# The first edge list sorted in two halves, the in-direction in two passes, and GpSimd's indirect DMAs held to two in flight

## The chip, the cores and the metric

The kernel runs on 1 core of one Trainium2 chip. The metric is the device time of one execution in microseconds, as the median of several runs.

## The reference, cut to what matters

A layer over a graph of 6250 nodes and 100000 edges, then a mixture of six experts. `hidden` is the layer-normalised x:

```python
def _srgnn_conv(x, W, b, src, dst, num_nodes):
    xl = x @ W.T + b
    msgs = xl[src]
    agg = jax.ops.segment_sum(msgs, dst, num_segments=num_nodes)
    cnt = jax.ops.segment_sum(jnp.ones((src.shape[0],), x.dtype), dst, num_segments=num_nodes)
    return agg / jnp.maximum(cnt, 1.0)[:, None]
input_in = _srgnn_conv(hidden, W_in, b_in, src, dst, n)
input_out = _srgnn_conv(hidden, W_out, b_out, dst, src, n)
gi = jnp.concatenate([input_in, input_out], axis=-1) @ W_ih.T + b_ih
gh = hidden @ W_hh.T + b_hh
# three gates from gi and gh (sigmoid, sigmoid, tanh) give the new rows
x = x + gru(gi, gh, hidden)
x = x + experts(_layernorm(x))   # 6 experts, the best 2 of each token
```

## The kernel before, in words

Everything is written out for the engines by hand, with semaphores; each engine runs its own list of instructions in order.

Nodes are padded to 6400 = 50 buckets (`NB`) of 128. Edges are 782 tiles (`TILES`) of 128, in room for 784 slots (`NS`); `HS` = 392 is half of that. For each direction the kernel needs the edges in the order of the receiving node. `positions(d)` (VectorE L900 and L942, TensorE L1553 and L1580) works out the place of each edge. A place is a slot (a tile) and a row in it. Then the list is written into order in one of two ways:

- A **sort tile**: VectorE builds a one-hot of the rows times the payload (L974, two of 128x128) and, VectorE (L978) or ScalarE (L614), a step over the slots (128x788). TensorE adds rows x steps into PSUM, 4 matmuls of 393 columns a tile (L1600). `decode` takes differences of neighbouring columns and gets the entries back.
- A **scatter**: GpSimd writes 128 entries into a list in DRAM by an indirect DMA (L392).

The list of direction 0 (the in-direction) takes 448 tiles (`SORTED_TILES`) by a loop of sort tiles, 112 groups of 4, and 336 by scatters, beside positions(1); SP reads the scattered list back and `decode(0)` adds both. The list of direction 1 is sorted inside the in-direction, three sort tiles a visit.

Then each direction gathers and sums. GpSimd gathers the 128 sender rows of a tile by an indirect DMA into a ring (L431, 782 a direction). Four tiles are a batch. A bucket may begin in the middle of a batch, so TensorE makes 245 **visits** (batch, bucket) a direction. In a visit VectorE builds the one-hot of the four tiles (L1070), and TensorE multiplies it with each tile's rows (L1674, 512 columns, the high and the low halves of the values) and with ones for the count (L1675). `bucket_mean` ends a bucket: ScalarE scales the high half (L606 `hi_mean`), VectorE adds the low half (L1100, L1171).

In the out-direction each bucket is followed by the products of the gates and the routing for that tile, and the experts come last, with 108 gathers (L448) and 108 adding scatters (L459) of GpSimd.

TensorE's sequencer runs register instructions (addresses that depend on loop counters) and waits between the matmuls. GpSimd's gathers wait for `slot_done`, which a visit's last matmul signals.

Of the kernel before, what the change touches and what calls it, by code (L numbers as in the profile page):

```python
# [13 lines left out]
F32 = mybir.dt.float32  # L14
# [26 lines left out]
VISITS = BATCHES - 1 + NB  # L41
KEY = 256
SORTED_TILES = 448
TILES = -(-EDGES // P)
VISIT_TILES = 3
GROUP = 4
# [5 lines left out]
SORT_GROUPS = SORTED_TILES // GROUP  # L52
# [3 lines left out]
ACT_TILES = (1, 3)  # L56
LIST = 2 * NS * P
# [14 lines left out]
MORE = TILES - VISITS * VISIT_TILES  # L72
# [13 lines left out]
assert MORE == NB - 3 and SORT_GROUPS % SETS == 0 and NB % 4 == 2  # L86


def gnn_moe_program(nc, x, edges, w, out, table, lists, means, routed):
    ctx = ExitStack()  # L90
    with ctx:
# [41 lines left out]
        def twin_sb(name, shape):  # L133
# [18 lines left out]
        bucket_base = sb("bucket_base", [P, 1], F32)  # L152
        base_digit = sb("base_digit", [P, 2], F32)
        base_row = carve("sort", [2 * HALF])
        count_digits = sb("count_digits", [P, 2], F16)
        bucket_i = sb("bucket_i", [P, 4], I32)
# [7 lines left out]
        slot_of, row_of, pay_hi, pay_lo = [[carve(user, [NS]) for user in ("sort", "live")] for _ in range(4)]  # L164
        list_at = carve("sort", [NS], I32)
        payload = carve("sort", [2, NS], I32)
        raw_list = list_at
        late = at["live"]
        step_gap = carve("live", [NS])
        first_slot = sb("first_slot", [P, 2], F32)  # L170
        first_place = sb("first_place", [P, 2], F32)
        first_batch = sb("first_batch", [1, 2, 64], I32)
        first_row = carve("sort", [64], I32)
# [7 lines left out]
        assert 4 * (at["live"] - LIVE) - 2 * 4 * NS >= WIDE_RING * 4 * D  # L181
# [22 lines left out]
        ring = sb("ring", [P, RING, 2 * D], F16)  # L204
        rings = (ring[:], over(region_at + 4 * LIVE, [WIDE_RING, 2 * D], F16))
# [93 lines left out]
        names = ("consts const_step spread_ready edges_in ln_mean ln_stats rows_scaled h_ready hi_ready split_ready table_stored "  # L299
                 "dve_step onehot_ready onehot_used slots16_ready slot_prefix_ready base_ready "  # L300
                 "list_at_ready list_zeroed list_in  merged sort_ready sort_used sort_summed column_ready half_ready receivers_ready "
                 "decoded  turn owners_marked owners_summed rows_landed slot_done "
                 "node_onehot_used key_ready node_onehot_ready bucket_done inv_ready hi_mean_ready "
# [8 lines left out]
        ln_in = [sem(f"ln_in{i}") for i in range(2)]  # L312
        spill_landed = [sem(f"spill_landed{i}") for i in range(2)]
        x_landed = [sem(f"x_landed{i}") for i in range(2)]
        S = {n: sem(n) for n in names}
        scatter_landed = sem("scatter_landed")
# [3 lines left out]
        N_CONSTS = 21  # L320
        sums, counts = (banks[4], banks[6]), (banks[5], banks[7])
        sort_hi, sort_lo = banks[0:2], banks[2:4]
        owners = banks[4:6]
# [12 lines left out]

        block = ctx.enter_context(nc.Block())

        @block.gpsimd
        def _(pool):  # L340
            g = nc.gpsimd
            c = S["consts"]
# [12 lines left out]
            g.memset(first_batch[:], BATCHES - 1).then_inc(c, 1)  # L355
# [32 lines left out]
            pool.wait_ge(S["list_zeroed"], 12 * 16)  # L388
            pool.wait_ge(S["list_at_ready"], 1)

            for t_ in range(SORTED_TILES, NS):
                g.indirect_dma_start(  # L392
                    out=lists[0][:], out_offset=bass.IndirectOffsetOnAxis(ap=list_at[:, t_:t_ + 1], axis=0),
                    in_=payload[:, 0, t_:t_ + 1], in_offset=None,
                ).then_inc(scatter_landed, 16)

# [25 lines left out]
            for d in range(2):  # L422
                pool.wait_ge(S["decoded"], 2 * d + 1)
                for i in range(TILES):
                    if i == LEAD:
                        pool.wait_ge(S["decoded"], 2 * d + 2)
# [13 lines left out]
            pool.wait_ge(S["iters_ready"], 1)  # L440
            pool.wait_ge(S["xn_landed"], (NB // 2 + 1) * 16)
# [3 lines left out]
            def gather_tokens(i):  # L445
                par, k = i // STREAMS % 2, i % STREAMS
                for h in range(2):
                    g.indirect_dma_start(  # L448
                        out=rows[:, par, k, h, :], out_offset=None, in_=routed[:],
                        in_offset=bass.IndirectOffsetOnAxis(ap=token[:, 2 * i + h:2 * i + h + 1], axis=0),  # L450
                    ).then_inc(rows_in[par][k], 16)

            def add_results(i):
# [4 lines left out]
                for h in range(2):  # L458
                    g.indirect_dma_start(  # L459
                        out=out[:], out_offset=bass.IndirectOffsetOnAxis(ap=token[:, 2 * i + h:2 * i + h + 1], axis=0),  # L460
                        in_=result[:, i % STREAMS, h, :], in_offset=None, compute_op=ALU.add,
                    ).then_inc(S["added"], 16)
# [10 lines left out]
        def _(sp):  # L473
# [6 lines left out]
            entries = lists[0].rearrange("(p n) o -> p (n o)", p=P)[:, 0:NS]  # L480
            for q in range(4):
                sp.dma_start(entries[:, q * (NS // 4):(q + 1) * (NS // 4)],
                             zeros16[:, 0:NS // 2].bitcast(I32)).then_inc(S["list_zeroed"], 16)

            for q in range(2):
                sp.dma_start(means[NP + q * P:NP + q * P + P, :], zeros16[:].bitcast(F32)
                             ).then_inc(S["list_zeroed"], 16)
                sp.dma_start(out[NP + q * P:NP + q * P + P, :], zeros16[:].bitcast(F32)
                             ).then_inc(S["list_zeroed"], 16)
                sp.dma_start(routed[NP + q * P:NP + q * P + P, 0:D], zeros16[:].bitcast(F32)  # L490
                             ).then_inc(S["list_zeroed"], 16)
                sp.dma_start(routed[NP + q * P:NP + q * P + P, D:ROW], zeros16[:, 0:2 * (ROW - D)].bitcast(F32)
                             ).then_inc(S["list_zeroed"], 16)
# [14 lines left out]

            sp.wait_ge(scatter_landed, (NS - SORTED_TILES) * 16)
            sp.dma_start(raw_list, entries).then_inc(S["list_in"], 16)  # L510
            sp.wait_ge(S["list_in"], 16)

            sp.wait_ge(S["decoded"], 2)
            sp.dma_start(r_w1, w["r_w1"].rearrange("(c p) n -> p c n", p=P)).then_inc(S["experts_in"], 16)
            sp.dma_start(e_b3.rearrange("p e d -> p (e d)"), w["e_b3"].to_broadcast([P, NE * D])).then_inc(S["experts_in"], 16)
            for n, name in enumerate(("e_w1", "e_w2", "e_w3")):
                sp.dma_start(e_w[n].rearrange("p e c m -> p (e c) m"), w[name].rearrange("e (c p) n -> p (e c) n", p=P)
                             ).then_inc(S["experts_in"], 16)
            for d in range(2):
# [7 lines left out]
                with sp.Fori(0, whole) as r:  # L527
                    for k in range(parts):
                        landed(r, k)
# [5 lines left out]
        def _(act):  # L535
# [68 lines left out]
            def hi_mean_step(q, k):  # L604
                act.wait_ge(S["inv_ready"], q)
                a.activation(hi_mean[:], sums[k][:, 0:D], ACT.Copy, scale=inv_count[:, 1:2]  # L606
                             ).then_inc(S["hi_mean_ready"], 1)

# [4 lines left out]
            def slot_steps(d, t, out_):  # L613
                a.activation(out_, iota_half, ACT.Sign, scale=-1.0, bias=slot_of[d][:, bass.ds(t, 1)]  # L614
                             ).then_inc(S["column_ready"], 1)

            act.wait_ge(S["half_ready"], 1)
            act.wait_ge(S["merged"], 2 * NB + 4)
            with act.Fori(0, SORT_GROUPS // SETS) as r:
                for g_ in range(SETS):  # L620
                    act.wait_ge(S["sort_used"], r * SETS + (g_ + 1))
                    act.sem_inc(S["turn"], 1)
                    for k in ACT_TILES:
                        slot_steps(0, r * SORT_BUFS + (g_ * GROUP + k), slot_step[:, g_ * GROUP + k, :])
            act.wait_ge(S["decoded"], 2)

            def spill_mean(j, k):
                hi_mean_step(j + 1, k)
# [4 lines left out]
            def visit_step(j, b, past):  # L633
                at_ = b + j
                act.wait_ge(S["node_onehot_used"], at_ + (OH + 1 - SETS))
                act.sem_inc(S["turn"], 1)
                slot_steps(1, at_ * VISIT_TILES + (past + 1),
                           slot_step[:, bass.ds(at_ * GROUP % SORT_BUFS + 1, 1), :].rearrange("p a m -> p (a m)"))

            def bucket_steps(j, k, more, later=True):  # L640
                act.sem_inc(S["turn"], 1)
                lo = act.value_load(first_batch[0:1, 0, bass.ds(j, 1)], min_val=0, max_val=BATCHES - 1)
                hi = act.value_load(first_batch[0:1, 0, bass.ds(j + 1, 1)], min_val=0, max_val=BATCHES - 1)
                past = j + 1 if more else MORE
                visit_step(j, lo, past)
                if later:
                    spill_mean(j - 1, 1 - k)
                act.sem_inc(S["turn"], 1)
                with act.If(hi > lo):
                    with act.Fori(lo + 1, hi + 1) as b:  # L650
                        visit_step(j, b, past)
# [1315 lines left out]
```

## Time and profile before

| what | value |
|---|---|
| median of 3 runs | 3091.45 us (3090.6 to 3100.2) |
| span of the profiled execution | 4434.5 us |
| mean granted clock of TensorE in it | 0.808 |

The profiled execution is known by its span alone, which is 1343 us over the median of the runs. Parts of it: the front with positions and scatters up to about 560 us, the sort loop up to about 880, the in-direction up to about 2300, the out-direction up to about 3950, the experts to the end.

### The profile page before, as it was taken

To read this page: it belongs to the slowest core of one execution; us is meant where nothing else is said; L and a number is where in the kernel's file an instruction comes from. 1 tells how busy PE (TensorE), PEld (TensorE's weight loads), DVE (VectorE), ACT (ScalarE), POOL (GpSimd) and SP (SyncE) were. 2 spreads that over 40 slices of the span, in tenths; PEclk is the share of its full clock that TensorE was granted. 3 is DMA by queue.
4 is the path that set the end of the run, shared out by engine and by line. 5 is a ranking of instruction groups with operands and counts; after the bars stand their busy time and mean duration, and the time that the engine had idled before them with its cause. 6 is when DMAs were issued, how large, how long until landed. Compare 5 with 4: busy or idle time off the path is not lost. (4 is left out here: it accounts for less than half of the span.)

```text
span 4434.5 us, 68226 instructions
## 1 busy us (share of the span) xinstructions
PE 2745.1 (62%) x14312; PEld 1616.8 (36%) x14313; DVE 2093.1 (47%) x6910; ACT 908.1 (20%) x1572; POOL 2164.5 (49%) x2165
## 2 busy tenths in 40 slices
PE   5211159977777777777764555555555555566896
PEld 2100025533333333333322333333333333345775
DVE  8201179975565556655552333443333433354221
ACT  4100026631112111111110010110111101112443
POOL 0777700035665555655645444444444444433786
PEclk9655589988888888888877777777777777787998
DMA  3100000022222222222222222222222222212444
GB/s 116 30 24 24 18 16 0 0 95 80 86 81 82 78 79 81 79 83 81 84 72 83 77 82 72 74 79 74 83 72 76 75 75 82 71 60 45 80 80 61
DMA packets 178175, 298.24 MB, mean 67 GB/s; under 512 B 51779, under 2 KB 123460, under 8 KB 178118
## 3 DMA queue, kind: packets, MB, share of 16 engines
q0 software_dynamic: 106560, 234.06, 19.8%
q10 hardware_dynamic: 44790, 35.90, 2.6%
q1 hardware_dynamic: 26768, 27.70, 2.0%
q14 instruction: 43, 0.35, 0.0%
q8 instruction: 14, 0.23, 0.0%
HBM read 255.56 MB, written 41.94 MB: 67 GB/s over the span
## 5 line engine op out<-in xcount | busy, mean ns | idle before, releaser
L431 POOL DMA_INDIRECT ring<-split_rows,live x782 | 791.5, 1012 | 923.4 <-DVE live L1035 381.8
L431 POOL DMA_INDIRECT over<-split_rows,gather_row x782 | 747.5, 956 | 933.0 <-PE bank L1674 681.5
L1600 PE MATMUL bank<-over,over 128*128 (+1 forms) x4920 | 1008.9, 354 | 143.1 <-issue 123.6
L1600 PEld LDWEIGHTS bank<-over,over 128*128 (+1 forms) x4920 | 485.9, 102 | 597.7 <-issue 351.9
L974 DVE TENSOR_SCALAR over<-iota_cols,live,live 128x128 f16 x1564 | 411.4, 319 | 119.9 <-issue 113.1
L392 POOL DMA_INDIRECT list<-sort,sort x336 | 332.7, 990 | 218.3 <-issue 111.0
L1674 PE MATMUL bank<-ring,dense 128*128 x980 | 329.5, 430 | 126.7 <-issue 100.1
L1714 PE MATMUL bank<-dense,dense 128*128 128x512 f32 (+1 forms) x600 | 262.0, 437 | 184.5 <-DVE dense L1183 174.1
L1675 PE MATMUL bank<-ones_col,dense 128*128 128x1 f16 x1960 | 334.9, 171 | 2.7 <-issue 2.5
L1674 PE MATMUL bank<-over,dense 128*128 x980 | 277.7, 386 | 94.5 <-issue 77.8
L614 ACT ACTIVATE over<-live,live 128x788 f16 x245 | 221.6, 945 | 492.2 <-remote 271.7
L606 ACT ACTIVATE hi_mean<-bank,inv_count 128x256 f32<-128x256 f32 x100 | 47.4, 474 | 1331.4 <-DVE inv_count L1097 586.9
L1733 PE MATMUL bank<-ident,mean_b 128*128 128x128 f32 x100 | 30.4, 400 | 432.5 <-DVE mean_b L1171 345.3
L1161 DVE TENSOR_SCALAR inv_count<-bank 128x1 f32<-128x1 f32 x50 | 7.9, 158 | 586.9 <-remote 536.7
L614 ACT ACTIVATE over<-live,sort 128x788 f16<-128x788 f16 x224 | 200.6, 944 | 200.7 <-DVE sort L942 102.9
L1715 PE MATMUL bank<-w_gate_low,dense 128*128 128x512 f32 (+1 forms) x600 | 239.7, 400 | 0.0
L978 DVE TENSOR_SCALAR over<-iota_cols,live 128x788 f16 x537 | 230.1, 428 | 19.3 <-issue 18.6
L1716 PE MATMUL bank<-dense,dense 128*128 128x512 f32 (+1 forms) x600 | 238.0, 397 | 0.0
L1070 DVE TENSOR_TENSOR dense<-live,node_key 128x512 f32 x245 | 168.9, 689 | 138.6 <-issue 51.1
L974 DVE TENSOR_SCALAR over<-iota_cols,sort,sort 128x128 f16<-128x128 f16 x896 | 227.1, 308 | 13.9 <-DVE live L965 0.5
L1714 PEld LDWEIGHTS bank<-dense,dense 128*128 128x128 f32 x600 | 146.2, 244 | 217.7 <-DVE dense L1183 180.0
L1889 PE MATMUL bank<-over,over 128*128 128x256 f32 x864 | 204.8, 401 | 29.7 <-issue 27.3
(304 smaller groups left out, 3927.7 us busy)
## 6 DMA issues: line engine op xcount, KB each, us to landing
norm<-in_x SPq DMA_DIRECT2D x20, 640.0 KB
ring<-split_rows,live POOLq DMA_INDIRECT x782
over<-split_rows,gather_row POOLq DMA_INDIRECT x782
split_rows<-over SPq DMA_DIRECT2D x10, 640.0 KB
in_edge_means<-dense ACTq DMA_DIRECT2D x50, 128.0 KB
dense<-in_x ACTq DMA_DIRECT2D x50, 128.0 KB
dense<-in_edge_means ACTq DMA_DIRECT2D x50, 128.0 KB
out<-dense ACTq DMA_DIRECT2D x25, 256.0 KB
```

What stands on the lines that cost most here:

```text
L392: g.indirect_dma_start(out=lists[0][:], out_offset=bass.IndirectOffsetOnAxis(ap=list_at[:, t_:t_ + 1], axis=0), in_=payload[:, 0, t_:t_ + ...
L431: g.indirect_dma_start(out=rings[d][:, i % ring_slots[d], :], out_offset=None, in_=table[:], in_offset=bass.IndirectOffsetOnAxis(ap=gather ...
L614: a.activation(out_, iota_half, ACT.Sign, scale=-1.0, bias=slot_of[d][:, bass.ds(t, 1)]).then_inc(S["column_ready"], 1)
L974: ins = e.tensor_scalar(rows_(half), iota_cols[:, 0:P], row_of[d][:, bass.ds(t, 1)], pay[:, bass.ds(t, 1)], ALU.is_equal, ALU.mult)
L978: ins = e.tensor_scalar(slots, iota_cols[:], slot_of[d][:, bass.ds(t, 1)], 2.0, ALU.is_le, ALU.mult)
L1600: ins = t.matmul(bank[h][:, 0:HS + 1], rows_(half), slots(h), start=False, stop=False, skip_group_check=True)
L1674: summed = t.matmul(sums[k][:, :], oh, rows, start=False, stop=False, skip_group_check=True)
L1675: ins = t.matmul(counts[k][:, 0:1], oh, ones_col[:], start=False, stop=False, skip_group_check=True)
L1714: t.matmul(o, a_hi, b_hi, start=first, stop=False, skip_group_check=True)
L1715: t.matmul(o, a_hi, b_lo, start=False, stop=False, skip_group_check=True)
L1716: return t.matmul(o, a_lo, b_hi, start=False, stop=last, skip_group_check=True)
L1889: ins = t.matmul(stream_bank[k][:, m * 2 * P:(m + 1) * 2 * P], w_stage[:, k, n_, c, m * P:m * P + P], right[:, k, c, :], start=(c == 0), s ...
```

## The change

- No scatters. The list of direction 0 is sorted in two halves of 392 slots each. A sort tile of it takes two matmuls of 393 columns. The first 392 tiles are sorted in a loop (`half_group`, 98 groups of 4) ahead of the in-direction.
- The in-direction is made in two passes of 147 visits each, 294 in all. Pass 0 works on the first half of the list, and meanwhile the other 390 tiles (`late_groups`, `late_tiles`, `late_steps`: 10 for each of the first 39 buckets) are sorted; decode(1) and receivers(1) follow in pass 0. Pass 0 writes a bucket's sums to DRAM (`bucket_part`, `spill_part`), pass 1 loads and completes them (`load_part`, `bucket_mean`).
- Pass 0 sorts two tiles of direction 1 a visit, pass 1 three.
- A sort tile's payload rows are built by one instruction of 128x256. In the half loop three of four slot steps are ScalarE's.
- A visit's two halves of the values are added in PSUM: per tile a matmul of 256 columns and one of 257, where the last column is a one that stands in the ring; no L1675, and no `hi_mean` in the out-direction.
- `few_queued`: each indirect DMA of GpSimd waits until the last but one has left its engine.

The core of the diff:

```diff
-SORTED_TILES = 448
+HALF_TILES = TILES - HS
 VISIT_TILES = 3
+EARLY_TILES = 2
+BUCKET_TILES = 10
-ACT_TILES = (1, 3)
+ACT_TILES = (1, 2, 3)
+SLOT = 2 * D + 8
+SENT_AHEAD = 2
...
+            def few_queued():
+                issued[0] += 1
+                if issued[0] > SENT_AHEAD:
+                    pool.wait_ge(S["sent"], issued[0] - SENT_AHEAD)
...
+                    if d == 0 and i == HS:
+                        pool.wait_ge(S["decoded"], 3)
                     if i % BATCH == 0 and i >= ring_slots[d]:
                         pool.wait_ge(S["slot_done"], d * NS + i + BATCH - ring_slots[d])
+                    few_queued()
                     g.indirect_dma_start(
-                        out=rings[d][:, i % ring_slots[d], :], out_offset=None, in_=table[:],
+                        out=rings[d][:, i % ring_slots[d], 0:2 * D], out_offset=None, in_=table[:],
                         in_offset=bass.IndirectOffsetOnAxis(ap=gather_row[d][:, i:i + 1], axis=0),
+                        engine_sem=S["sent"],
                     ).then_inc(ring_landed[d][i // BATCH % (ring_slots[d] // BATCH)], 16)
...
+            def sort_rows(d, t, rows_):
+
+                return e.scalar_tensor_tensor(
+                    out=two(rows_), in0=iota_cols[:, 0:P].rearrange("p (o m) -> p o m", o=1).to_broadcast([P, 2, P]),
+                    scalar=row_of[d][:, bass.ds(t, 1)],
+                    in1=pay[d][:, bass.ds(t, 1), :].rearrange("p t (a o) -> p (t a) o", o=1).to_broadcast([P, 2, P]),
+                    op0=ALU.is_equal, op1=ALU.mult)
...
+            def half_products(rows_, slots):
+                for bank, half in ((half_hi, 0), (half_lo, 1)):
+                    ins = t.matmul(bank[:, 0:HS + 1], rows_(half), slots, start=False, stop=False,
+                                   skip_group_check=True)
+                return ins
...
+            def late_groups(j):
+                for q in range(BUCKET_GROUPS):
+                    for i in range(2):
+                        pe.wait_ge(S["half_ready"], j * BUCKET_TILES + (HS + 2 * q + i + 1))
+                        pe.wait_ge(S["half_column"], j * BUCKET_TILES + (HALF_GROUPS * len(ACT_TILES) + 2 * q + i + 1))
+                        pe.sem_inc(S["turn"], 1)
+                        buf = late_buffer(j * BUCKET_GROUPS + q, i)
+                        ins = half_products(lambda half: row_payload[:, buf, half * P:half * P + P
...
                     for q in range(BATCH):
...
+                        for lo_, hi_ in ((0, D), (D, 2 * D + 1)):
...
                     if d == 0:
-                        for i in range(VISIT_TILES):
-                            ins = sort_tile(at_ * VISIT_TILES + (past + i), i, at_)
+                        for i in range((EARLY_TILES, VISIT_TILES)[p]):
+                            ins = sort_tile(visit_tile(p, at_, past) + i, i, at_)
```

GpSimd's instructions ahead of and at the start of the gathers, before the change (`list` is the list in DRAM, `split_rows` the table of rows, `sort_79` and `live_82` the buffers with the places):

```order
L385 AFFINE_SELECT spread_base<-spread_base 128x50 [waits spread_ready]
L392 DMA list<-sort_79,sort_78 200704x1 [waits list_at_ready,list_zeroed]
L392 DMA list<-sort_79,sort_78 200704x1 x335
L431 DMA ring<-split_rows,live_82 128x512 [waits decoded,fold_done,table_stored]
L431 DMA ring<-split_rows,live_82 128x512 x15
L431 DMA ring<-split_rows,live_82 128x512 [waits slot_done]
```

and the same place after it (`sent` is the new semaphore, `slot_done` frees the ring):

```order
L409 AFFINE_SELECT spread_base<-spread_base 128x50 [waits spread_ready]
L439 MEMSET ring 128x16 [waits decoded,fold_done,table_stored]
L450 DMA ring<-split_rows,live_79 128x512 x2
L450 DMA ring<-split_rows,live_79 128x512 [waits sent] x14
L450 DMA ring<-split_rows,live_79 128x512 [waits sent,slot_done]
L450 DMA ring<-split_rows,live_79 128x512 [waits sent] x3
```

The 336 scatters are gone, and each gather has a wait for `sent` of its own beside the wait for the ring at every fourth.

The first two of the four edge tiles in TensorE's visit, in the in-direction, before (`ring` is the gathered rows, `dense_104` the one-hots; ISA is a register instruction):

```order
L1688 ISA
L1674 ISA [waits node_onehot_ready,rows_landed]
L1674 ISA
L1674 MATMUL bank<-ring,dense_104 128x512
L1675 MATMUL bank<-ones_col,dense_104 128x1
L1674 ISA
L1674 MATMUL bank<-ring,dense_104 128x512
L1675 MATMUL bank<-ones_col,dense_104 128x1
```

and after:

```order
L1841 ISA
L1825 ISA [waits node_onehot_ready,rows_landed]
L1825 ISA
L1825 MATMUL bank<-ring,dense_101 128x256
L1825 ISA
L1825 MATMUL bank<-ring,dense_101 128x257
L1825 ISA
L1825 MATMUL bank<-ring,dense_101 128x256
L1825 ISA
L1825 MATMUL bank<-ring,dense_101 128x257
```

Five register instructions stood at the products of a visit, and nine stand there now, one ahead of each matmul; the two matmuls of a tile have 256 and 257 columns for 512 and 1.

## Rows read from the trace of the kernel before

**Rows 1.** Head of the page: span; engine, busy us (share), instructions.

```profile
span 4434.5 us, 68226 instructions
...
PE 2745.1 (62%) x14312; PEld 1616.8 (36%) x14313; DVE 2093.1 (47%) x6910; ACT 908.1 (20%) x1572; POOL 2164.5 (49%) x2165
```

**Rows 2.** Table by stretches: busy us of each engine, granted clock, DMA share, GB/s.

```profile
core 0: us, PE busy (x) PEld busy (x) DVE busy (x) ACT busy (x) POOL busy (x), PEclk, DMA share, GB/s
...
114.00:340.00 226.00, 42.78 (x140) 18.06 (x138) 34.57 (x82) 26.70 (x46) 170.21 (x173) 0.57 0.10 27
340.00:560.00 220.00, 26.50 (x79) 10.67 (x79) 35.22 (x61) 15.28 (x24) 162.51 (x164) 0.52 0.08 21
...
660.00:880.00 220.00, 220.00 (x1312) 127.04 (x1310) 209.23 (x827) 147.03 (x164) 0.00 (x0) 1.00 0.00 0
...
1000.00:2200.00 1200.00, 900.73 (x4678) 411.83 (x4675) 700.46 (x2310) 223.94 (x265) 710.70 (x701) 0.86 0.28 81
...
2400.00:3900.00 1500.00, 821.80 (x4458) 549.58 (x4458) 592.73 (x2187) 167.39 (x348) 667.49 (x700) 0.78 0.25 77
```

**Rows 3.** Waits from 114 to 560 us: line <- releaser, us in total, times, longest.

```profile
DVE over L900 <- remote: 168.5, 9, 21.0
...
DVE sort L942 <- remote: 127.6, 7, 19.5
```

**Rows 4.** Waits from 2400 to 3900 us, the same columns.

```profile
POOL over L431 <- PE bank L1674: 640.8, 47, 16.3
DVE inv_count L1161 <- remote: 522.1, 41, 18.6
```

**Rows 5.** Order of time, 2996 to 3012 us: start, duration, instruction, idle before, releaser.

```profile
2997.97 0.27 PE L1735 MATMUL bank<-ident,flags 128*128 128x128 f32 x1
...
3006.70 0.95 POOL L431 DMA_INDIRECT over<-split_rows,gather_row  x1 [0.30 <-issue]
3010.27 0.42 DVE L1180 CAST dense<-bank 128x256 fp32r<-128x256 f32 x1 [9.81 <-remote]
```

**Rows 6.** Line L392: count, shortest/median/longest ns, first and last start.

```profile
L392 POOL DMA_INDIRECT list<-sort,sort x336: 954/962/2474, 114.7 to 557.4; - x168
```

**Rows 7.** GpSimd in order of time, two neighbours: start, duration.

```profile
300.29 0.95 POOL L392 DMA_INDIRECT list<-sort,sort  x1 [0.30 <-issue]
301.55 0.96 POOL L392 DMA_INDIRECT list<-sort,sort  x1 [0.30 <-issue]
```

**Rows 8.** The page's groups for two sort steps: count | busy us, mean ns | idle.

```profile
L614 ACT ACTIVATE over<-live,sort 128x788 f16<-128x788 f16 x224 | 200.6, 944 | 200.7 <-DVE sort L942 102.9
...
L974 DVE TENSOR_SCALAR over<-iota_cols,sort,sort 128x128 f16<-128x128 f16 x896 | 227.1, 308 | 13.9 <-DVE live L965 0.5
```

**Rows 9.** Line L1100: count, shortest/median/longest ns.

```profile
L1100 DVE SCALAR_TENSOR_TENSOR dense<-bank,inv_count,hi_mean x50: 482/483/485, 984.0 to 2298.5; 128x256 f32<-128x256 f32 x50
```

**Rows 10.** TensorE in order of time, one visit of the in-direction.

```profile
1283.01 0.39 PE L1674 MATMUL bank<-ring,dense 128*128 x1 [0.48 <-issue]
...
1283.99 2.17 PE L1600 MATMUL bank<-over,over 128*128 x12
1286.59 0.39 PE L1674 MATMUL bank<-ring,dense 128*128 x1 [0.42 <-issue]
```

**Rows 11.** TensorE in order of time, one visit of the out-direction.

```profile
2712.84 0.39 PE L1674 MATMUL bank<-over,dense 128*128 x1 [0.44 <-issue]
...
2714.39 0.39 PE L1674 MATMUL bank<-over,dense 128*128 x1 [0.44 <-issue]
```

**Rows 12.** Line L1674: shortest/median/longest ns, first and last start.

```profile
L1674 PEldq FUSED_REGOPS  x2450: 3/74/1374, 957.8 to 3987.5; - x189
...
L1674 PE MATMUL bank<-ring,dense x980: 376/377/634, 958.1 to 2294.9; 128*128 x196
...
L1674 PE MATMUL bank<-over,dense x980: 376/376/607, 2314.4 to 3988.1; 128*128 x196
```

**Rows 13.** TensorE's groups, 1000 to 2200 us: busy us, mean ns | idle before.

```profile
L1600 PE MATMUL bank<-over,over 128*128 x2802 | 632.1, 367 | 126.0 <-issue 112.8 <-DVE over L978 7.2 <-DVE over L974 2.3
...
L1657 PE MATMUL bank<-zeros 128*128 128x512 f16 x44 | 21.9, 499 | 65.6 <-issue 65.6
```

**Rows 14.** The page's groups for the gathers and for hi_mean.

```profile
L431 POOL DMA_INDIRECT ring<-split_rows,live x782 | 791.5, 1012 | 923.4 <-DVE live L1035 381.8
...
L606 ACT ACTIVATE hi_mean<-bank,inv_count 128x256 f32<-128x256 f32 x100 | 47.4, 474 | 1331.4 <-DVE inv_count L1097 586.9
```

More of the change, by code:

```diff
@@ L526, in _ @@
                 whole = (BATCHES - 1) // parts
-                with sp.Fori(0, whole) as r:
+                begun = 0
+                if d == 0:
+                    begun = -(-HALF_BATCHES // parts)
+                    with sp.Fori(0, begun) as r:
+                        for k in range(parts):
+                            landed(r, k)
+                    load_experts()
+                with sp.Fori(begun, whole) as r:
                     for k in range(parts):
@@ L641, in bucket_steps @@
+            def bucket_steps(p, j, k, pair=0, more=False, half=False, later=True):
                 act.sem_inc(S["turn"], 1)
[L642 to L643 removed]
+                lo = act.value_load(first_batch[0:1, p, bass.ds(j, 1)], min_val=0, max_val=BATCHES - 1)
+                hi = act.value_load(first_batch[0:1, p, bass.ds(j + 1, 1)], min_val=0, max_val=BATCHES - 1)
@@ L650, in bucket_steps @@
                     with act.Fori(lo + 1, hi + 1) as b:
-                        visit_step(j, b, past)
-            bucket_steps(0, 0, True, False)
+                        visit_step(p, j, b, past)
+            bucket_steps(0, 0, 0, half=True, later=False)
+            for first, last, half in ((0, HALF_BUCKETS // 2, True), (HALF_BUCKETS // 2, NB // 2 - 1, False)):
+                with act.Fori(first, last) as r:
+                    for k in (1, 0):
+                        bucket_steps(0, r * 2 + (2 - k), k, r, half=half)
+            bucket_steps(0, NB - 1, 1, NB // 2 - 1)
+            spill_part(NB - 1, 1, NB // 2 - 1)
+            for k in range(2):
+                act.wait_ge(spill_landed[k], NB // 2 * 16 + 16)
+            bucket_steps(1, 0, 0, more=True, later=False)
             for n_ in range(4):
@@ L931, in positions @@
-                e.tensor_copy(first_slot[:, d:d + 1], bucket_i[:, 1:2])
-                e.tensor_copy(first_place[:, d:d + 1], bucket_i[:, 2:3])
+                                              prefix[:, HS - 1:HS] if h and d else 0.0, ALU.mult, ALU.add))
+                for n_ in range(parts):
+                    end = NS - 1 if n_ == parts - 1 else HS - 1
+                    ins = e.tensor_copy(bucket_i[:, n_:n_ + 1], prefix[:, end:end + 1])
+                step(ins)
+                e.tensor_single_scalar(bucket_i[:, 2:2 + parts], bucket_i[:, 0:parts], 7, ALU.arith_shift_right)
@@ new lines, in positions @@
+                for n_ in range(parts):
+                    hi_at, lo_at = n_ * HALF, (parts + n_) * HALF
+                    ins = e.scalar_tensor_tensor(out=first_row[0:1, n_, 0:NB], in0=base_row[0:1, hi_at:hi_at + NB],
+                                                 scalar=float(P), in1=base_row[0:1, lo_at:lo_at + NB],
+                                                 op0=ALU.mult, op1=ALU.add)
+                step(ins)
+                if d == 0:
+                    step(e.tensor_single_scalar(first_row[0:1, 0, 0:NB], first_row[0:1, 0, 0:NB],
+                                                float(HS * P - 1), ALU.min))
@@ new lines, in decode, with receivers @@
+                v.wait_ge(S["decoded"], (2, 3, 5)[p])
+            def receivers(p):
+                d = p // 2
+                s2 = decode_rooms[d][2]
+                v.wait_ge(S["owners_summed"], p + 1)
+                for h, bank in enumerate(owners[p]):
+                    at_ = HS if p == 1 else h * HS
+                    step(e.scalar_tensor_tensor(out=receiver[d][:, at_:at_ + HS], in0=bank[:, 0:HS],
+                                                scalar=float(KEY), in1=s2[:, at_:at_ + HS], op0=ALU.mult, op1=ALU.add))
@@ L1130, in _ @@
             e.memset(bias_pack.bitcast(F32), 0.0).then_inc(S["bias_clear"], 1)
-            bucket_a(0, True)
+            bucket_a(0, False)
+            for n_ in range(4):
+                with v.Fori(EARLY_PAIRS[n_], EARLY_PAIRS[n_ + 1]) as r:
+                    for k in (1, 0):
+                        next_bucket(0, r * 2 + (2 - k), k, r, half=n_ == 0)
+                if n_ == 1:
+                    decode(1)
+                if n_ == 2:
+                    receivers(1)
+            next_bucket(0, NB - 1, 1, NB // 2 - 1)
+            bucket_part(NB - 1, 1, NB // 2 - 1)
+            bucket_a(1, True)
             for n_ in range(4):
```

613 lines of the change are left out of this document (344 added, 269 removed).

## Prediction

> **What bounds the kernel now.** I read the head of the page first: the profiled execution took 4434.5 us, TensorE was busy for 62% of it and GpSimd for 49% [rows 1]. The median of the runs shown is 3091.45 us, 1343 us less. No engine fills the span, so I went to the table by stretches [rows 2]. The reader is to see two kinds of stretch there. From 660 to 880 us TensorE is busy for all of its 220 us at a granted clock of 1.00: the sort loop. From 114 to 560 us, where GpSimd issues the scatters, TensorE, VectorE and ScalarE together are busy for 42.8 + 34.6 + 26.7 + 26.5 + 35.2 + 15.3 = 181 us of 446. So for at least 265 us none of the three works. In the out-direction, 2400 to 3900 us, TensorE has 822 us of 1500.
>
> The waits say what stands there. In the scatter stretch VectorE's L900 and L942 wait 168.5 and 127.6 us for a releaser on another engine that the trace does not place, up to 21.0 us at a time [rows 3]. In the out-direction VectorE's L1161 waits 522.1 us in the same way, and GpSimd's gathers 640.8 us for the matmuls that free the ring [rows 4]. One place shows the pattern: TensorE's L1735 starts at 2997.97 and lasts 0.27 us; VectorE's L1180, which needs only that product, starts at 3010.27 after 9.81 us of idling, and in between GpSimd goes through one gather after another until its last at 3006.70 [rows 5]. TensorE's signal comes through late while GpSimd has indirect DMAs queued. That is what holding the DMAs back would act on.
>
> **How the profiled time stands to the timed one.** Take out the 265 us and the 522 us, and add that without the first the sort loop would run beside the scatters and not after them (another 300 us). Those three are 1087 of the 1343 us by which the profiled execution is longer, and the in-direction's own stretch (from 958.1 to 2294.9 [rows 12], 1337 us, against about 1000 us by the price of its parts, below) covers the rest. So the timed runs cannot hold much of these late signals: what is left without them is about the median. I therefore make the sum for the timed runs from the durations of undisturbed stretches, start at 3091, and treat late signals in the timed runs as a rival.
>
> **Front: scatters out, half a list in.** The scatters run from 114.7 us, 336 of them [rows 6], one each 1.26 us by two neighbours [rows 7], so 425 us: they end at 540 (in the trace, with some longer ones, the last starts at 557.4). Beside them positions(1) should take about as long as positions(0), which was done with the load and the layer norm by 114.7: 125 us, to 240. The sort loop issues 1312 matmuls in the full 220 us, 16 a group, so 2.68 us a group [rows 2]; 112 groups are 300 us, to 540. Both paths end together there. After the change the scatters, their landing and the read-back are gone, and the loop has 98 groups. The new row builder is one scalar_tensor_tensor of 128x256. Nothing in the trace is the same operation; the nearest are L1100, 128x256 from PSUM at 0.483 us, and the pair of tensor_scalars that it replaces at 227.1/896 = 0.253 us each, 0.51 us a pair [rows 8, 9]. A group costs VectorE 4 x 0.40 to 0.48 plus one step of half the width, about 0.2 us: 1.8 to 2.1 us. ScalarE's three half-width steps are 3 x 0.944/2 = 1.42 us, TensorE's eight matmuls 1.34. So 98 x 1.85 = 181 us, to about 420: **-120 us** (-95 to -130). The first decode handles half the columns: **-10**.
>
> **In-direction: 294 visits for 245, and 390 late tiles.** At full clock a visit starts at 1283.01, its four edge tiles end at 1283.99, the twelve sort matmuls take 2.17 us, and after 0.42 us of idle "issue" the next starts at 1286.59: 3.58 us [rows 10]. In the out-direction, with no sort tiles, visits stand 1.55 us apart with 0.44 us of "issue" [rows 11]. So each visit has about 0.43 us in which the array waits for its sequencer. At L1674 the trace has 2450 register instructions for 490 visits, five a visit, with a median of 74 ns [rows 12]; after the change the code has nine. Four more at 0.074 us are 0.30 us; in proportion to the gap they are 4 x 0.43/5 = 0.34, which I take (an estimate; nothing if matmuls cover them).
>
> Before: 245 x 3.58 = 877, 50 bucket turns of 1.5 us (65.6 us of idle in 44 at L1657 [rows 13]) 75, 49 extra sort tiles 33: 985 us. GpSimd's 782 gathers at 1.012 us plus 0.30 of issue make 1026 at most, or 990 at the usual 0.96 [rows 7, 14]. The two are even; I take 1000.
>
> After, pass 0: a visit has two sort tiles, 3.58 - 0.68 + 0.34 = 3.24 us, 147 of them 476. A late tile has two matmuls of 393 columns, 0.34 us at the rate of the sort tiles, and its own waits and register work, between nothing and 0.45 us; half of that gives 0.57, 390 of them 222. Turns 75. Sum 773. Pass 1: 147 x 3.92 = 576, 47 extra tiles 32, turns 75: 683. Together 1456, **+456**. With no register time added, 147 x 2.90 + 133 + 75 and 147 x 3.58 + 32 + 75: 634 + 633 = 1267, +267. If no idle "issue" shows at all, visits of 3.15 and two fewer for a sort tile: about 1140, +140. A longer bucket turn points up: at its end a sort matmul waits 126.0 us in all [rows 13], 2.9 us a bucket; if that is of the turn, 50 more turns add 143. VectorE, busy for 700.5 of 1200 us with three sort tiles a visit [rows 2], gets two in pass 0 and 390 x 0.48 = 187 us of late rows; GpSimd needs 391 x 1.26 = 493 us a pass. Neither becomes the bound. I take **+370**, between the two values that keep the gap seen in rows 10.
>
> [...] The trace shows 1.5 us of a turn without work for the array at L1657 [rows 13]; it doesn't show what the sequencer does in it. [...]
>
> **Out-direction and experts.** hi_mean's ACT step (0.474 us, 50 of its 100 [rows 14]) leaves the chain: -24. The visits get the same four register instructions: 245 x 0.34 = +83 if TensorE is the limit there; it is busy for 822 of 1500 us, and the chain through VectorE and ScalarE decides part of it. I take **+20** (-24 to +60). The hold on GpSimd costs nothing as long as two DMAs in flight keep it busy: 1.26 us apart, with 0.30 of it issue.
>
> Sum: 3091 - 120 - 10 + 370 + 20 = 3351, **3350 us**. In a profile the late signals should go: the front ends near 440 us where it ended at 880, the in-direction is 1456 - 1337 = 120 us longer, and the out-direction about 500 shorter. Its span should fall to 4434 - 440 + 120 - 500, about 3610 us, although the timed runs get longer.
>
> **Rivals.**
> 1. Faster: late signals are in the timed runs too. 787 us of them are in the trace (265 and 522). The change loses 260 by my sum, so the balance turns where a third of the 787 is in the timed runs; with half, 3350 - 394 = 2956 us. For it: the hold acts on just that pattern, and the scatters that caused the first part are gone. Against it: the accounting above leaves little room for them in 3091 us. Chance 0.22.
> 2. Faster or no change: TensorE's register work is hidden. Then the in-direction costs +140, the out-direction -24: 3091 - 130 + 140 - 24 = 3077; with gathers that the profile slows, even less. For it: TensorE's share of the in-direction is 75% by the table (900.7 of 1200 us). Against: the gap stands in each full-clock visit. Chance 0.16, 0.09 of it faster.
> 3. Slower still: the hold makes GpSimd wait for a late signal of its own. If each indirect DMA starts 0.30 us later, a pass of 391 is 610 us, still under TensorE's; in the out-direction 782 x 0.30 = +235 at most: 3585. Against: a limit of two leaves the next one queued. Chance 0.05.
> 4. My forecast, chance 0.57.
>
> **How the numbers follow.** About 0.3% (9 us) is what a measurement of this kernel can tell from no change. Slower: 0.57 + 0.05 = 0.62. Faster: 0.22 + 0.09 = 0.31. Same: the other 0.07 of rival 2. The forecast's own range is 3190 (in-direction +210) to 3500 (+500 with longer turns). The whole range goes down to 2930, where rival 1 has half of the late signals, and up to 3500.
>
> **What would show it.** In the profile after: no long VectorE waits without a placed releaser in the front; the half sort loop at about 1.85 us a group and done some 120 us sooner after positions(1); full-clock visits at about 3.2 and 3.9 us with 0.7 to 0.8 us of "issue"; late tiles at 0.57 us; the two passes together over 1300 us; gathers still 1.26 us apart. The forecast is wrong if visits without sort work keep 1.55 us, if both passes together are near 1050 us, or if the timed median falls although the passes are long: then the late signals were in the timed runs.

## The result, and the profile after

The changed kernel takes 3616.3 us (median of 4 runs, 3609.5 to 3621.3) where the kernel before takes 3091.0 us: a ratio of 1.169, with an interval of 1.1665 to 1.1712. It is 525 us slower. The direction was forecast and the size was not: 260 us were forecast, and the time lies outside the range.

The head of the page of the changed kernel, and its two groups of gathers:

```profile
span 3619.3 us, 77644 instructions
...
PE 2775.0 (77%) x14673; PEld 1664.5 (46%) x14674; DVE 2141.5 (59%) x6095; ACT 1100.0 (30%) x2031; POOL 1921.9 (53%) x1832
...
L450 POOL DMA_INDIRECT ring<-split_rows,live x782 | 857.2, 1096 | 815.1 <-PE bank L1825 333.6
L450 POOL DMA_INDIRECT over<-split_rows,gather_row x782 | 772.5, 988 | 241.8 <-DMA over<-split_rows,gather_row 184.2
```

The span is 3619 us, and this time it is the time of the runs too. The span before was 4434 us against runs of 3091 [rows 1]. So the two pages can't be subtracted: they would show a kernel that became 815 us faster. What the profile of before was is the first thing to find out (e0, e1 below). In the first group the gathers of the in-direction stand idle for 815 us, in the second one for 242.

The changed kernel by stretches. They are cut at the zeroing products of TensorE that open a bucket, so that they are the front, pass 0 (25 buckets with gathers, then 13 with late tiles alone, then the last 12), pass 1 (24 buckets without gathers, then 26 with), and the out-direction; the experts follow to the end:

```profile
core 0: us, PE busy (x) PEld busy (x) DVE busy (x) ACT busy (x) POOL busy (x), PEclk, DMA share, GB/s
0.00:444.00 444.00, 324.82 (x1476) 118.86 (x1478) 414.16 (x935) 263.93 (x581) 18.29 (x45) 0.93 0.18 57
444.00:1093.00 649.00, 495.72 (x2504) 238.26 (x2501) 340.75 (x813) 240.85 (x372) 382.39 (x384) 0.95 0.29 83
1093.00:1258.00 165.00, 110.69 (x492) 46.64 (x492) 85.70 (x219) 79.62 (x142) 0.00 (x0) 0.93 0.03 10
1258.00:1329.00 71.00, 46.16 (x221) 23.95 (x221) 33.16 (x89) 9.81 (x11) 12.93 (x14) 0.83 0.39 125
1329.00:1526.00 197.00, 128.65 (x622) 68.41 (x623) 109.43 (x332) 38.45 (x48) 2.47 (x3) 0.85 0.11 34
1526.00:2134.00 608.00, 475.05 (x2615) 258.63 (x2613) 377.33 (x968) 128.40 (x156) 455.63 (x383) 0.94 0.33 94
2134.00:3190.00 1056.00, 854.34 (x5179) 621.36 (x5179) 674.83 (x2469) 167.36 (x343) 767.53 (x790) 0.94 0.41 121
```

The in-direction runs from 444 to 2134 us, 1690 us. From 1093 to 1526 us GpSimd has 17 instructions, 14 of them ahead of pass 1: the edges come sorted by receiver, so the first half of the list has the edges of the first 24 buckets and part of the 25th alone. Pass 0 finds no gathers for the last 25, and pass 1 none for the first 24; each of them still gets a visit.

### The profile page after: what moved, and what is told of

It is laid out like the page before. It is cut to its first block and busy times, and to the rows that moved or that the text cites. A ratio compares the mean times of both kernels' runs of the same rounds, so it can differ in the third digit from the quotient of the medians.

```text
span 3619.3 us, 77644 instructions
## 1 busy us (share of the span) xinstructions
PE 2775.0 (77%) x14673; PEld 1664.5 (46%) x14674; DVE 2141.5 (59%) x6095; ACT 1100.0 (30%) x2031; POOL 1921.9 (53%) x1832
## 5 line engine op out<-in xcount | busy, mean ns | idle before, releaser
L1716 PE MATMUL bank<-over,over 128*128 x3128 | 633.4, 346 | 84.1 <-DVE over L1049 44.9
L1730 PE MATMUL bank<-over,over 128*128 128x393 f16 (+1 forms) x1564 | 396.3, 362 | 143.0 <-issue 118.7
L1042 DVE SCALAR_TENSOR_TENSOR over<-iota_cols,sort,sort 128x256 f16<-128x256 f16 (+1 forms) x782 | 333.3, 497 | 250.7 <-PE bank L1730 250.0
L634 ACT ACTIVATE over<-live,sort 128x393 f16 (+1 forms) x684 | 368.9, 613 | 320.3 <-PE bank L1730 270.6
L1716 PEld LDWEIGHTS bank<-over,over 128*128 x3128 | 310.2, 100 | 336.0 <-issue 246.4
L1825 PEld LDWEIGHTS bank<-ring,dense 128*128 x2352 | 232.4, 99 | 353.3 <-issue 256.0
L1042 DVE SCALAR_TENSOR_TENSOR over<-iota_cols,live,live 128x256 f16 x782 | 362.1, 478 | 31.0 <-PE bank L1716 29.4
L1825 PEld LDWEIGHTS bank<-over,dense 128*128 x1960 | 199.7, 102 | 290.8 <-issue 205.9
L1730 PEld LDWEIGHTS bank<-over,over 128*128 128x128 f16 (+1 forms) x1564 | 124.2, 98 | 414.1 <-issue 310.5
L483 POOL DMA_INDIRECT out<-over,dense x108 | 173.4, 1606 | 79.7 <-ACT over L869 22.8
```

The source lines that it names most:

```text
L634: a.activation(out_, iota_half[:, 0:number], ACT.Sign, scale=-1.0, bias=slot_of[d][:, bass.ds(t, 1)]).then_inc(ready, 1)
L1042: return e.scalar_tensor_tensor(out=two(rows_), in0=iota_cols[:, 0:P].rearrange("p (o m) -> p o m", o=1).to_broadcast([P, 2, P]), scalar=r ...
L1716: ins = t.matmul(bank[h][:, 0:HS + 1], rows_(half), slots(h), start=False, stop=False, skip_group_check=True)
L1730: ins = t.matmul(bank[:, 0:HS + 1], rows_(half), slots, start=False, stop=False, skip_group_check=True)
L1825: ins = t.matmul(bank[:, 0:hi_ - lo_], oh, rows, start=False, stop=False, skip_group_check=True)
```

## The experiments

The kernel before was timed again beside each group of runs, with medians from 3091 to 3104 us. So a difference in us between two kernels of different groups is good to about 12 us; the ratios are each to the kernel before of the same group.

**e0: the kernel before, profiled once more.**

> The kernel before once more, for its profile. If queued indirect DMAs of GpSimd always delay TensorE's signals in a profiled execution, the span is again near 4430 us with VectorE's long unplaced waits. If that was a matter of the one execution shown, the span is near 3100, and the hold had nothing to take away.

Its span is 3093.3 us. Head of its cores, then its stretches, cut as above: in-direction from 582 to 1626, where the first bucket of the out-direction is opened, out-direction to 2664, experts:

```profile
core 0: 3093.3 us, clock 0.941
```

```profile
582.00:1626.00 1044.00, 848.17 (x5247) 428.89 (x5248) 763.82 (x2621) 251.89 (x301) 787.20 (x784) 0.98 0.38 110
1626.00:2664.00 1038.00, 844.68 (x5030) 562.27 (x5028) 675.64 (x2454) 190.52 (x389) 768.65 (x790) 0.93 0.41 123
2664.00:3093.00 429.00, 338.55 (x1574) 287.64 (x1574) 109.12 (x288) 172.62 (x384) 283.79 (x216) 0.88 0.42 68
```

No wait in it is put down to a releaser that the trace does not place. VectorE's longest in the out-direction (1700 to 2600 us) is now short, and for TensorE:

```profile
DVE inv_count L1161 <- PE bank L1691: 106.2, 43, 6.4
```

The late signals of [rows 3 to 5] belonged to the one profiled execution shown. A second profiled execution of the same kernel, at 3093.3 us, has none. All comparisons from here are with this trace. In it the gathers of both directions run back to back (the page's groups):

```profile
L431 POOL DMA_INDIRECT ring<-split_rows,live x782 | 786.2, 1005 | 245.1 <-issue 234.1
L431 POOL DMA_INDIRECT over<-split_rows,gather_row x782 | 774.3, 990 | 256.3 <-issue 232.7
```

That is 786 + 245 = 1031 us for each direction, nearly all of it without a wait for another engine. So the gathers set the pace of both directions. In the in-direction TensorE is close behind: it waits 39.8 us for gathered rows (the releaser is SP, which passes their landing on), and GpSimd 4.0 us for it:

```profile
PE bank L1674 <- SPq L524: 39.8, 44, 4.6
POOL ring L431 <- PE bank L1674: 4.0, 13, 0.3
```

**e1 and e2: the hold alone, and the change without it.** Each has the hold's two lines put in or taken out at each indirect DMA; e1:

```diff
+                    few_queued()
                     g.indirect_dma_start(
...
+                        engine_sem=S["sent"],
```

> The kernel before with the hold of the change alone, on its scatters, gathers and the experts' DMAs. If the added 525 us are the two passes' own work and the late signals belong to the profiled execution alone, the timed median stays within 1% of 3091 us, and the profiled span comes down to about it, with the in-direction at about 1000 us and the scatters ending near 540. If the hold is what costs, the timed median goes up by 150 to 300 us. If late signals are in the timed runs as well, it falls below 3000.

> The changed kernel without the hold. If the passes cost and the hold is free, the timed median stays within 1% of 3616 us while the profiled span goes back up, to over 4000. If the hold costs, the timed median falls to about 3350, my forecast. If late signals matter in timed runs, it rises.

e1: 3103.6 us, a ratio of 1.0032 (1.0014 to 1.005). e2: 3612.0 us, 1.1661 (1.1627 to 1.1694), which overlaps that of the change. Its profiled span is 3610 us, not over 4000 as I expected: without the hold there are no late signals either. So the hold costs 4 to 15 us of the kernel before and gives nothing back; all but that of the 525 us is the rest of the change. The rival that the hold costs is out.

**e4: four more register instructions a visit, in the kernel before.**

```diff
-                        rows = batches[:, bass.ds(part, 1), q * 2 * D:(q + 1) * 2 * D].rearrange("p a m -> p (a m)")
-                        summed = t.matmul(sums[k][:, :], oh, rows, start=False, stop=False, skip_group_check=True)
+                        for lo_, hi_ in ((0, D), (D, 2 * D)):
+                            part_rows = batches[:, bass.ds(part, 1), q * 2 * D + lo_:q * 2 * D + hi_].rearrange("p a m -> p (a m)")
+                            summed = t.matmul(sums[k][:, lo_:hi_], oh, part_rows, start=False, stop=False,
+                                              skip_group_check=True)
```

> The kernel before with the hold, and each 512-column product of a visit made as two of 256 columns, each with its own register instruction: four more register instructions and four more matmuls a visit in both directions, 490 visits. If register instructions cost what I took (0.34 us a visit), the in-direction gets 83 us longer and the out-direction up to 83: 90 to 170 us over the kernel with the hold alone. If they are hidden, within 30 us of it.

3220.0 us, 116 over e1. The zeroing products of two neighbouring buckets, in e0 and in e4 (last two times: first and last start):

```profile
L1657 PE MATMUL bank<-zeros x2: 387/388/388, 707.7 to 728.3; 128*128 128x512 f16 x2
```

```profile
L1672 PE MATMUL bank<-zeros x2: 387/388/388, 817.0 to 840.1; 128*128 128x512 f16 x2
```

A bucket of the in-direction goes from 20.6 to 23.1 us, 0.5 us for each of its 4.9 visits. The array has the same columns to take in, so this is the price of four matmuls and their register instructions in TensorE's own row; no run parts the two. It is not hidden there, and it is more than the 0.34 us of the forecast. From the first zeroing product to the first of the out-direction e1 takes 1043 us and e4 1149:

```profile
L1672 PE MATMUL bank<-zeros x51: 377/387/607, 583.1 to 1626.4; 128*128 128x512 f16 x51
```

```profile
L1672 PE MATMUL bank<-zeros x51: 383/388/608, 584.6 to 1733.8; 128*128 128x512 f16 x51
```

That is 106 us of the 116 (less than 245 x 0.5, since e1's TensorE has waits for gathered rows to give away: 33.9 us in e1, 4.8 in e4). What follows, with the same four more a visit in the out-direction, gets about 6 us longer (3215.3 - 1733.8 for 3102.1 - 1626.4). From the first gather of the out-direction to the last it is 1014 us in e4 and 1017 in e1: behind the gathers the four more are hidden.

**e3 and e8: without the late tiles,** in the changed kernel and in the spread one:

```diff
             def late_groups(j):
+                return
...
-                    pe.wait_ge(S["half_used"], HALF_GROUPS + SETS + HALF_BUCKETS * BUCKET_GROUPS)
+                    pe.wait_ge(S["half_used"], HALF_GROUPS + SETS)
```

and the same `return` in `late_tiles` and `late_steps`.

> The changed kernel without the 390 late tiles: the second half of the list is left out, so pass 1 sums wrong rows. The trace of the changed kernel has a late tile each 0.76 us where it stands alone. If TensorE's row of late tiles is the bound, 390 x 0.76 = 296 us go: about 3320. By my forecast's price of 0.57 it would be 222 us. If they lay beside other work, under 100 us go.

> The spread kernel without its 390 late tiles: the second half of the list is left out, so pass 1 sums wrong rows. If late tiles are fully on the path when the work is spread, 296 us under the spread kernel. If they fall behind the gathers (391 x 1.32 = 516 us a pass), under 200.

e3: 3458.0 us, 158 less; neither number that I gave. In its trace the first 25 buckets fall from 26.3 to 21.5 us only, since there the gathers are next in line (15.6 a bucket, some 20.6 us by the 1031 us for 782), and the later buckets of pass 1, whose gathers all read one row here, take 27.4 us for 23.5, for a reason that is not settled. e8, where no bucket has more gathers than TensorE's work covers, is cleaner: 3251.1 us, 286 under e5. A late tile costs 286/390 = 0.73 us, near the 0.76 of the trace and not the 0.57 of the forecast.

**e5: the tiles dealt out to the halves.**

```diff
-    edges = _np.ascontiguousarray(edges.reshape(2, NS, P).transpose(2, 0, 1))
+    order = [*range(0, TILES - 1, 2), TILES - 1, *range(1, TILES - 1, 2), TILES, TILES + 1]
+    edges = _np.ascontiguousarray(edges.reshape(2, NS, P)[:, order].transpose(2, 0, 1))
```

> The changed kernel with the tiles of the input list dealt out alternately to the two halves (an order of the array on the host), so that each pass has gathers for all 50 buckets; before it the first 25 buckets had all of pass 0's gathers, since the list comes sorted by receiver. Visits and sort tiles stay in number. If GpSimd's standing idle through the single-visit buckets is the loss (25 x 5.3 + 25 x 8.3 = 340 us), the time falls by 200 us or more. If TensorE's count of visits, late tiles and turns is the bound in every bucket, passes of 147 x 3.39 + 390 x 0.76 + 50 x 2 = 894 and 147 x 3.92 + 32 + 50 x 2.5 = 733 follow: about 60 us less, 3550.

3537.3 us, ratio 1.1387 (1.1364 to 1.1411): 79 less, near the 3550 of the theory that TensorE's count of things is the bound, and far from the 200 or more of the other. Bucket openings in pass 0 of the changed kernel (with gathers and late tiles; late tiles alone; neither), in pass 1 (without gathers; with), then of the spread kernel in pass 0 and 1, and of e8 in pass 0:

```profile
L1805 PE MATMUL bank<-zeros x3: 272/272/272, 889.4 to 942.0; 128*128 128x257 f16 x3
L1805 PE MATMUL bank<-zeros x4: 272/272/272, 1092.8 to 1130.8; 128*128 128x257 f16 x4
L1805 PE MATMUL bank<-zeros x4: 273/282/376, 1258.4 to 1274.2; 128*128 128x257 f16 x4
L1805 PE MATMUL bank<-zeros x4: 282/282/283, 1402.2 to 1427.0; 128*128 128x257 f16 x4
L1805 PE MATMUL bank<-zeros x2: 281/282/282, 1631.7 to 1655.2; 128*128 128x257 f16 x2
```

```profile
L1805 PE MATMUL bank<-zeros x3: 272/272/272, 615.0 to 653.8; 128*128 128x257 f16 x3
L1805 PE MATMUL bank<-zeros x3: 281/282/283, 1389.0 to 1418.5; 128*128 128x257 f16 x3
```

```profile
L1808 PE MATMUL bank<-zeros x3: 281/281/282, 604.3 to 628.0; 128*128 128x257 f16 x3
```

The buckets of the changed kernel take 26.3, 12.7, 5.3, 8.3 and 23.5 us; in the spread one 19.4 and 14.8, and 11.9 without late tiles. In a spread pass GpSimd has about 8 gathers a bucket, some 10 us at 1031/782 us each, so it sets no bucket's time. GpSimd's pause in the changed kernel is mostly a consequence: what TensorE does in it would have to be done at another time anyway.

**e7 and e9: late tiles' waits once a pair,** in the changed kernel and in the spread one.

```diff
-                    for i in range(2):
-                        pe.wait_ge(S["half_ready"], j * BUCKET_TILES + (HS + 2 * q + i + 1))
-                        pe.wait_ge(S["half_column"], j * BUCKET_TILES + (HALF_GROUPS * len(ACT_TILES) + 2 * q + i + 1))
-                        pe.sem_inc(S["turn"], 1)
+                    pe.wait_ge(S["half_ready"], j * BUCKET_TILES + (HS + 2 * q + 2))
+                    pe.wait_ge(S["half_column"], j * BUCKET_TILES + (HALF_GROUPS * len(ACT_TILES) + 2 * q + 2))
+                    pe.sem_inc(S["turn"], 1)
+                    for i in range(2):
```

> The changed kernel with the waits of a late tile done once for two tiles on TensorE. A late tile takes 0.76 us in the trace, 0.34 of it matmuls. If the rest is TensorE's own waits and register work, one set of waits less a pair saves 0.2 to 0.35 us of it where late tiles are the bound: 30 to 60 us of 3616. If VectorE or ScalarE sets the pace of late tiles (two steps of 0.51 us a pair on each), nothing.

> The changed kernel with both edits: tiles dealt out to the halves, and late tiles' waits done once a pair. If in every bucket TensorE's visits, late tiles and turns add up, the two gains add: 3616 - 79 - 68 = about 3470, with pass 0 near 820 us. If the gain of one lay in the same waits as that of the other, it stays over 3500. Neither theory has it under the kernel before.

e7: 3547.9 us, 68 less, 0.35 us a pair, a little over the 60 that I gave as the most. TensorE in order of time, in the changed kernel and in e7:

```profile
1136.66 0.51 PE L1730 MATMUL bank<-over,over 128*128 x2 [2.16 <-issue]
1137.41 0.49 PE L1730 MATMUL bank<-over,over 128*128 x2 [0.24 <-issue]
1138.18 0.50 PE L1730 MATMUL bank<-over,over 128*128 x2 [0.27 <-issue]
```

```profile
1109.39 0.90 PE L1730 MATMUL bank<-over,over 128*128 x4 [2.16 <-DVE over L1042]
1110.57 1.68 PE L1730 MATMUL bank<-over,over 128*128 x5 [0.27 <-issue]
```

Two late tiles take 1.52 us with a set of waits each, and 1.18 with one. So the waits and their register values, 0.34 us, were most of the 0.42 that a late tile took beside its matmuls. The row builders and steps of VectorE and ScalarE nearly keep up: over the late tiles TensorE waits 23.3 and 6.6 us for the two in e7, 3.5 and 5.4 in the changed kernel. e9: 3464.1 us, ratio 1.1168 (1.1131 to 1.1204). The gains of 79 and 68 add up (3469 by the sum) to within what separates one group of runs from another, as they should where one engine's row is the bound. It is still 363 us over the kernel before.

**e10: another share of scatters in the kernel before.** `SORTED_TILES = 464` for 448.

> The kernel before with 464 tiles sorted and 320 scattered, for 448 and 336. In its clean profile the sort loop is over at 552 us and VectorE then waits 25.8 us for the scattered list, which is read back at 567 to 570.5. 16 scatters less are 16 x 1.26 = 20 us, four groups of the loop more are 4 x 2.68 = 11 us: the loop ends at about 563, ahead of it the list is in at about 550. If the front sets the time, 7 to 8 us go (0.25%); if the in-direction's later work covers it, nothing.

3094.0 us against 3101.1 us, ratio 0.9979 (0.9956 to 1.0001). It points the way that was expected and is not clear of no change. No run here is clearly faster than the kernel before.

## Why the prediction was right in its direction and wrong in its size

By the clean trace of before (e0) and the trace after, the terms of the sum measured:

| term | forecast, us | measured, us |
|---|---|---|
| front, with the first decode | -130 | 444 - 582 = -138 |
| in-direction | +370 | 1690 - 1044 = +646 |
| out-direction and experts | +20 | (3619 - 2134) - (3093 - 1626) = +18 |
| sum | +260 | +526 |

**The front was right,** nearly step by step. In e0 the scattered list is in 19 us after the sort loop ends (552 us), where the forecast had both paths end together:

```profile
570.52 0.26 DVE L1022 TENSOR_SCALAR live<-bank 128x96 f32<-128x96 f32 x1 [25.81 <-DMA sort<-list]
```

The half loop takes 1.82 us a group, for 1.85, by the steps that VectorE builds once a group:

```profile
300.03 0.34 DVE L1049 TENSOR_SCALAR over<-iota_cols,sort 128x393 f16<-128x393 f16 x1
301.84 0.34 DVE L1049 TENSOR_SCALAR over<-iota_cols,sort 128x393 f16<-128x393 f16 x1
```

**The step that failed is the in-direction's term,** "I take +370, between the two values that keep the gap seen in rows 10". Its working had three prices for TensorE's row, all of them low, and then took less than their sum:

- The taken value lay 86 us under the sum of the prices (456), on the chance that matmuls cover register work. Where TensorE's row is the bound they did not: four more matmuls with their register instructions took 0.5 us a visit in e4, and one set of waits with its register values 0.35 us a pair in e7.
- The row after came to 1690 us and not 1456, 234 more. Visits were priced at 3.24 and 3.92. They take 3.45 in pass 0 and 4.1 in pass 1, about 0.5 us over the visit of before for the same columns. In pass 1 it lies in the eight edge products: from the first of them to the first sort product it is 1.51 us, where it was 0.98 [rows 10], and from there to the next visit 2.62 for 2.60:

```profile
705.90 1.29 PE L1825 MATMUL bank<-ring,dense 128*128 x8 [0.46 <-issue]
...
709.35 1.28 PE L1825 MATMUL bank<-ring,dense 128*128 x8 [0.47 <-issue]
```

```profile
1656.91 1.30 PE L1825 MATMUL bank<-ring,dense 128*128 x8 [0.31 <-issue]
1658.42 2.21 PE L1716 MATMUL bank<-over,over 128*128 x12 [0.20 <-issue]
1661.04 1.28 PE L1825 MATMUL bank<-ring,dense 128*128 x8 [0.41 <-issue]
```

  That is about 147 x 0.2 x 2 = 59 us. Late tiles at 0.76 for 0.57 are 390 x 0.19 = 74. Turns of 1.5 us are the rest, about 100. In pass 0 a bucket of a single visit takes 5.3, so 5.3 - 3.45 = 1.9 us are its turn; in pass 1 it is 8.3 - 4.1 - 0.7 for the extra sort tile = 3.5 us. There the first sort tile of a bucket waits for VectorE, which comes to it only after ending the bucket before. In the 24 buckets without gathers these waits are 40.6 us:

```profile
PE bank L1716 <- DVE over L1049: 40.6, 23, 3.0
```

They begin like this:

```profile
1404.37 0.84 PE L1716 MATMUL bank<-over,over 128*128 x4 [1.93 <-DVE over L1049]
1405.61 1.89 PE L1825 MATMUL bank<-ring,dense 128*128 x8 [0.40 <-issue]
```

  The second row has eight edge products at 1.89 us for 1.28. The granted clock is 0.51 from 1405.5 to 1408 us, and 0.85 from 1329 to 1526. So the 3.5 us hold some of the clock too, how much is not shown. In the other 26 buckets of pass 1 TensorE waits 32.1 us for gathered rows. The rest of the 100 us is not divided up.

- The in-direction of before is 1044 us up to the first bucket of the out-direction, not 1000, which takes 44 back. 86 + 234 - 44 = 276, the whole of the miss in this term.

That edges sorted by receiver leave 25 buckets of pass 0 and 24 of pass 1 without gathers was not in the forecast at all. e5 prices it at about 80 us.

**The out-direction and the experts** came to +18 for the +20 taken, by luck: not in the way of the forecast, which shared the out-direction between TensorE and the chain through the other engines. Its gathers set the pace, before and after, with the same 1013 to 1015 us from the first to the last:

```profile
L431 POOL DMA_INDIRECT over<-split_rows,gather_row x782: 942/947/1474, 1616.0 to 2628.6; - x196
```

```profile
L450 POOL DMA_INDIRECT over<-split_rows,gather_row x782: 942/946/1466, 2124.6 to 3139.4; - x196
```

So the visits' register work (+83 if TensorE were the limit) is hidden, and the step that hi_mean leaves (-24) gives nothing back. The stretch takes 1056 for 1038 us, the experts an unchanged 429.

**The rivals.** Late signals in timed runs: there were none to take away, even in a second profile. Hidden register work: shown wrong by e4 for the in-direction (106 us longer), and right for the out-direction (about 6 us longer, with the experts). The hold that waits: e1 and e2 show it free to within 0.5% (a ratio of 1.0032 with it in the kernel before; 3612.0 us without it for 3616.3 in the changed one).

**The longer turns.** The prediction has 143 us for them, worked out from rows 13, in the upper end of its range and not in the +370. The turns did come out about 100 us longer, for the most part in pass 1, where the wait on VectorE shown above is part of it. What TensorE's sequencer does in a turn no trace shows in full. Transfers of instructions do not come with every turn: from 1329 to 1526 us, with 24 turns, the profile has 6:

```profile
q8 instruction: 2, 0.03, 0.1%
q14 instruction: 4, 0.03, 0.1%
```

In the whole span it has 70 (51 and 19), in e0 58 (44 and 14), 12 more for 50 more turns. What the 6 cost is not shown.

The forecast of the profiled span, 3610 us for 3619, hit for the wrong reason: it took the late signals off a span of 4434 us, and its in-direction was 234 us short while its out-direction and experts, 1714 us for 1485, kept more of the disturbed trace than they should.

## What to carry to other kernels

When the profiled span and the median of the runs differ as here, 4434 us for 3091, take another profile before pricing anything from it; the first one had 1340 us that neither the runs nor a second profile have. Where a row of small matmuls is the bound, count the instructions between them (waits, register values, addresses) at full price: four more matmuls for the same columns, with four more register instructions, cost 0.5 us a visit, and the second set of waits in a pair of late tiles 0.35 us. Where another engine sets the pace, as the gathers do in the out-direction, the same four matmuls and register instructions in each of 245 visits made the rest of the run 6 us longer. And a split into passes multiplies what is paid once a bucket (here 50 more turns, of 1.9 us in pass 0 and 3.5 in pass 1 where a bucket is a single visit); the 138 us won ahead were paid back more than four times in the in-direction.

## What the runs showed of the hardware that was not expected

In one profiled execution of the kernel before, VectorE waited up to 21.0 us at a time for releasers that the trace does not place, while GpSimd had indirect DMAs queued [rows 3, 5], at a mean granted clock of 0.808. Another of the same kernel had no such wait, at 0.941 and a span of 3093 us, and neither had the changed kernel without the hold, at 0.926 and 3610 us. What set the first one off is not settled.
